# Mixture-of-experts hand-over of an adaptive-layernorm transformer block: routing of the first sixteen tiles placed inside the last batch's attention steps, the last eight tiles handled in pairs

## The reference, cut to what matters

```python
h = _layernorm(x) * (1 + ca) + sa
x = x + ga * _L0_attn_ref(h, ...)          # q, k, v; softmax; z @ W_o.T + b_o
h = _layernorm(x) * (1 + cb) + sb
x = x + gb * _L0_ffn_ref(h, ...)

# _L0_ffn_ref
score = softmax(xf @ Wg + bg); gate = max(score); idx = argmax(score)
pos = sum((cumsum(onehot(idx), axis=0) - 1) * onehot)   # rank within its expert, in token order
keep = pos < cap                                        # cap = 256
buf[idx, pos] = xf                                      # only where keep
h = relu(buf @ W1[e] + b1[e]);  y = h @ W2[e] + b2[e]
out = where(keep, y[idx, pos] * gate, 0)
```

## Time and profile before

| | us |
|---|---|
| time, median of 3 runs | 1383.31 (1381.31 to 1388.11) |
| the profiled execution | 1389.05 |
| its span | 1387.2 |
| PE busy | 1235.2 (89%) |
| DVE busy | 824.6 (59%) |
| ACT busy | 573.5 (41%) |
| POOL busy | 326.3 (24%) |
| chain that ended last | PE 67%, issue 11%, ACT 6%, DMA 5%, DVE 5%, POOL 3% |

### The profile page before, as it was taken

The page is one execution under the profiler, slowest core; times in us unless marked ns, Lnnn a source line. Parts: engine busy times, 40 slices in busy tenths (PEclk is TensorE's granted clock), DMA queues, the critical chain, the costliest instruction groups (busy, mean ns, idle before and its releaser), DMA issues.

```text
span 1387.2 us, 24033 instructions
## 1 busy us (share of the span) xinstructions
PE 1235.2 (89%) x7258; PEld 864.4 (62%) x7258; DVE 824.6 (59%) x2163; ACT 573.5 (41%) x1387; POOL 326.3 (24%) x488
## 2 busy tenths in 40 slices
PE   4588888888999999999999999999988529999995
PEld 1455555655666666666666666666656428888884
DVE  6356666666667766666667666666655623444443
ACT  2245555545555555555555555555540001111110
POOL 3111121111233332222333212222212520111111
PEclk7689999999999999999999999999999759999998
DMA  5311112111221222122122211212257852565630
GB/s 188 129 66 58 66 57 80 50 38 44 78 71 64 69 78 73 54 68 79 57 72 66 82 54 61 76 53 68 76 183 261 271 182 87 196 235 174 232 103 18
DMA packets 100150, 139.29 MB, mean 100 GB/s; under 512 B 9980, under 2 KB 71294, under 8 KB 99968
## 3 DMA queue, kind: packets, MB, share of 16 engines
q1 hardware_dynamic: 91536, 113.55, 24.9%
q10 hardware_dynamic: 4464, 16.25, 2.9%
q0 software_dynamic: 4096, 8.82, 1.6%
HBM read 94.50 MB, written 48.00 MB: 103 GB/s over the span
## 4 chain that ended last, share of the span: by engine, by line
PE 67%; issue 11%; ACT 6%; DMA 5%; DVE 5%; POOL 3%; SPq 2%; DVEq 0%; ACTq 0%; POOLq 0%
PE SC L676 16%; PE Z L694 14%; PE Z L841 8%; PE SC L815 8%; ACT E L876 5%; PE XA L648 5%; PE XA L726 4%; PE XA L658 3%; PE XB L658 3%; DMA xln<-in_x 3%; PE XB L648 2%; POOL Wvl L1371 1%; PE XB L713 1%; DMA out<-th 1%; POOL slots_s L1476 1%
## 5 line engine op out<-in xcount | busy, mean ns | idle before, releaser
L876 ACT ACTIVATE E<-SC,nm 128x512 f32<-128x512 f32 (+7 forms) x512 | 375.1, 739 | 426.3 <-DVE nm L1089 426.3
L1089 DVE CUSTOM_DVE_ANT_0 SC<-SC,mask 128x512 f32<-128x512 f32 (+7 forms) x512 | 375.9, 786 | 205.4 <-PE SC L676 204.2
L676 PE MATMUL SC<-XQ,XK 64*128 64x512 f32 (+3 forms) x2304 | 270.0, 366 | 55.7 <-ACT E L876 54.1
L676 PEld LDWEIGHTS SC<-XQ,XK 64*128 64x128 f32 x2304 | 187.7, 190 | 155.5 <-issue 138.6
L694 PE MATMUL Z<-E,vs 128*64 128x512 f32 (+3 forms) x1536 | 271.9, 496 | 3.0 <-DVE vs L1067 3.0
L694 PEld LDWEIGHTS Z<-E,vs 128*64 128x64 f32 x1536 | 100.3, 138 | 140.9 <-issue 128.1
L841 PE MATMUL Z<-W,hh 128*128 128x256 f32 x512 | 114.9, 383 | 2.2 <-DVE yb L1335 2.2
L815 PE MATMUL SC<-bT,W 128*128 128x256 f32 x512 | 114.7, 383 | 0.0
L815 PEld LDWEIGHTS SC<-bT,W 128*128 128x128 f32 x512 | 98.5, 193 | 13.7
L841 PEld LDWEIGHTS Z<-W,hh 128*128 128x128 f32 x512 | 97.3, 192 | 15.6 <-DVE yb L1335 2.6
L876 ACT ACTIVATION_READ_ACCUMULATOR E<-SC,nm 128x1 f32 x512 | 101.1, 197 | 0.0
(11 more groups left out here) (191 smaller groups left out, 1720.7 us busy)
## 6 DMA issues: line engine op xcount, KB each, us to landing
W<-in_w SPq DMA_DIRECT2D x32, 1024.0 KB, 8.4
z_s<-zs ACTq DMA_DIRECT2D x31, 512.0 KB, 2.6
zt<-z_s SPq DMA_DIRECT2D x24, 512.0 KB, 3.8
W<-in_wqk SPq DMA_DIRECT2D x33, 257.0 KB, 2.7
slots_s<-zt SPq DMA_DIRECT2D x16, 520.0 KB, 3.9
xb<-slots_s SPq DMA_DIRECT2D x16, 520.0 KB, 3.7
xb<-xh_s SPq DMA_DIRECT2D x24, 256.0 KB, 4.7
Wv<-in_wv SPq DMA_DIRECT2D x17, 256.0 KB, 2.7
```

What stands on the lines that cost most here:

```text
L676: last = pe.matmul(SC[h][:, at:at + z - a], XK[rows, ap, kp, lo:lo + P], XQ[rows, ap, qp, a:z], start=(t == 0), stop=(t == 2))
L876: act.activation(E[:, h, EOFF[kb]:EOFF[kb + 1]], SC[h][:, at:at + S - lo], ACT.Exp, bias=nm[:, h, kb:kb + 1], scale=-1.0, accum_out=rs[:, ...
L1089: dve.tensor_tensor_reduce(SC[h][:, at:at + S - lo], SC[h][:, at:at + S - lo], mask[:, 0:S - lo], 1.0, BIG, ALU.add, ALU.min, nm[:, h, kb: ...
```

## The change

1. `TAIL` is 8 and `T0` is 24: tile 23 is a normal `post` tile, in step 32. In that step `weigh(LATE)` comes after the tile's projection, and `project_out(0)` follows at once. ACT copies `Z` to `zs` in two halves; the first needs only key blocks 0 to 3.
2. Tiles 0 to 15 (lot 0) are routed inside steps 25 (`PICK`) and 26 (`RANK`) of batch 3: fifteen DVE instructions placed among the step's own, one exponential on ACT, sixteen running sums of `oh` on POOL (`sum_lot`, into `before`), and two matmuls into `Z` on PE (`lot_ranks`), one with `tri` and `oh`, one with `ones` and `before`, added up in PSUM. The DVE sums `base` are gone.
3. Their rows are loaded by SP and scattered by POOL in four rounds of four tiles: the loads at the end of steps 26 to 29, the scatters at the start of steps 27 to 30, through the two buffers `lead`.
4. Batch 3's steps are written out instead of looped.
5. The hand-over routes lot 1 (tiles 16 to 23) and then the last eight in four pairs (`route_tail`), each with its own two small matmuls and 16 DVE instructions. POOL's powers 0, 1 and 2 stand ahead of `lot_scatter`, and each pair is scattered when it is routed.
6. The product `boB * GA` is added to `x` by POOL (`gate_bias`) in step 31, so `norm_tail` has one DVE instruction fewer. The constants of routing are made ahead of the steps.

```diff
-TAIL = TPB + 1
+TAIL = TPB
-GROUPS = [(0, 1)] + [(1 + 2 * k, 2) for k in range(TPB // 2)]
-LOTS = [(0, 2 * TPB), (2 * TPB, 3 * TPB), (3 * TPB, NT)]
+GROUPS = [(2 * k, 2) for k in range(TPB // 2)]
+LOTS = [(0, 2 * TPB), (2 * TPB, 3 * TPB)]
+PICK, RANK = (B - 1) * PAIRS + 1, (B - 1) * PAIRS + 2
+ROUNDS, LEAD = 4, 4
...
-    (3, 0, 4, (0, 1), ("late", "att", "proj", "post")),
+    (3, 0, 1, (0, 1), ("late", "att", "proj", "post")),
+    (3, 1, 2, (0, 1), ("late", "att", "proj", "post")),
+    (3, 2, 3, (0, 1), ("late", "att", "proj", "post")),
+    (3, 3, 4, (0, 1), ("late", "att", "proj", "post")),
     (4, 0, 1, (0,), ("late", "att", "post")),
-    (4, 0, 1, (1,), ("late",)),
+    (4, 0, 1, (1,), ("late", "post")),
...
+                n = round_at(st, RANK)
+                if n is not None:
...
+                        sp.wait_ge(lead_sent, 16 * LEAD * n)
+                    for k in range(2):
+                        t = LEAD * n + LEAD // 2 * k
+                        sp.dma_start(lead[k][:, :, 0:2 * D], xh_s[t:t + LEAD // 2].rearrange("t p d -> p t d")).then_inc(lead_in, 16)
...
+                n = round_at(st, RANK + 1)
+                if n is not None:
...
+                    pool.wait_ge(lead_in, 32 * (n + 1))
...
+                            pool.indirect_dma_start(slots_s, bass.IndirectOffsetOnAxis(slot_u[:, t:t + 1], 0), lead[k][:, q, :], None,
+                                                    bounds_check=NE * CAP - 1, oob_is_err=False).then_inc(lead_sent, 16)
...
+                    if v == 1 and at_step(st, RANK):
+                        pe.wait_ge(s["zevac"], st.of("zevac", 1))
+                        lot_ranks(0, Z)
+                    if not st.has("att") and st.has("late") and v == 2:
+                        weigh(LATE)
+                        project_out(0)
...
+            tail_pow(0)
+            sum_lot(1)
             tail_pow(1)
-            scatter(1)
             tail_pow(2)
-            pool.wait_ge(routed, 2)
-            scatter(2, (0,))
+            lot_scatter()
             tail_pow(3)
-            scatter(2, (1,))
-            tail_pow(4)
...
+            for n in range(len(GROUPS)):
+                tail_scatter(n)
```

More of the change, by code:

```diff
@@ L313, in adaln_block @@
         b2B = sb("b2B", [P, NW, D])
[L314 to L318, removed]
         assert top[0] <= place["hTh"]
@@ L717, in step @@
                             project(*piece)
-                    if st.has("late") and v == 0:
+                    if st.has("late") and st.has("att") and v == 0:
                         weigh(LATE)
@@ L742, in _, with turn @@
             pe.wait_ge(s["zevac"], TOTAL["zevac"])
[L744 to L759, removed]
+            def turn(n):
                 u0, size = GROUPS[n]
                 pe.wait_ge(tail_h2, n + 1)
+                if n > 0:
+                    pe.wait_ge(tail_tT, n)
                 for q in range(size):
@@ L774, in gate_logits, with ranks @@
                 last.then_inc(tail_gates, 1)
[L776 to L785, removed]
-            ranks(0)
[L788 to L793, removed]
+            def ranks(n):
+                if n > 0:
+                    pe.wait_ge(routed, n)
+                pe.wait_ge(onehot, n + 1)
+                k0 = LOTS[1][1] - LOTS[1][0]
+                pe.matmul(XB[:, 0:2 * NE], tri[:, :], oh[:, 0:2, :].rearrange("p q e -> p (q e)"), start=True, stop=False)
+                pe.matmul(XB[:, 0:2 * NE], ones[:, :], before[:, k0:k0 + 2, :].rearrange("p q e -> p (q e)"),
+                          start=False, stop=True).then_inc(prefix_mm, 1)
+            project_out(1)
+            turn(0)
+            project_out(2)
+            gate(0)
+            lot_ranks(1, XA)
+            turn(1)
+            project_out(3)
+            gate(1)
+            turn(2)
+            ranks(0)
+            gate(2)
+            turn(3)
             ranks(1)
[L795 to L798, removed]
+            gate(3)
             ranks(2)
-            pe.wait_ge(routed, len(LOTS))
+            ranks(3)
+            pe.wait_ge(routed, len(GROUPS))
             xbT = [XA, XB]
@@ L1422, in step @@
                         split_values_weights(st.b * COUPLES + st.j + 2)
+                if at_step(st, PICK):
+                    sum_lot(0)
+                if st.has("att") and not st.has("proj"):
+                    gate_bias()
             minus_halves = mhalf[:, :].broadcast_to([P, TPB])
@@ new lines, in lot_scatter @@
+            def lot_scatter():
+                pool.wait_ge(lot_slotted, 2)
+                for half in range(2):
+                    ks = range(half * HS // 2, (half + 1) * HS // 2)
+                    t = LOTS[1][0] + ks[0]
+                    for k in ks:
+                        pool.wait_ge(hs_in[k], 16)
+                    pool.tensor_copy(hs[:, ks[0]:ks[0] + HS // 2, 2 * D:ROW], ext[:, t:t + HS // 2, :]).then_inc(ext_ok, 1)
+                    pool.wait_ge(ext_ok, half + 1)
+                    for k in ks:
+                        t = LOTS[1][0] + k
```

418 lines of the change are left out of this document (273 added, 145 removed).

## The result

| | before | after |
|---|---|---|
| time, median (from to), 11 runs each | 1384.68 (1379.92 to 1388.86) | 1379.29 (1375.24 to 1381.99) |
| the profiled execution | 1389.05 | 1377.41 |
| its span | 1387.2 | 1375.6 |

The ratio is 0.9956, with a 95% interval of 0.9939 to 0.9974, and the medians lie 5.4 us apart where 21.7 were forecast. Both kernels were timed again in a later session, and there the ratio was 0.9947 (0.9928 to 0.9967) and the medians 7.4 us apart (1384.82 and 1377.43).

What follows compares the result with a forecast made beforehand. PE was taken to bound batch 3's steps, and the hand-over alone the time from 1040 to 1139. Hand-over gain 23.5 us less 1.8 for the steps gave 21.7, from 1383.31 to 1361.6 us, range 1353 to 1372.

Steps and rivals of the forecast that it cites:

- The last weighted sum: End of attention on PE: 2.4 us instead of 3.96, with 4.0 as the other bound.
- PE's projection of tile 23: End of attention: 3.72 us at full clock, filling most of PE's 2.75 us gap, so tile 23 costs nothing there.
- the fourth power: Hand-over: it stands behind POOL's 12.2 us of `lot_scatter`, so DVE waits some 5 us for it.
- The three routings: Hand-over, pairs 1 to 3: 5.8, 4.7 and 4.0 us, together 14.5, bounds 12 and 19.
- From the last routing to the experts: End of the hand-over: two scatters remain instead of eight, 7.6 us less, so 8.7 instead of 16.33.
- rival 1: DVE slows POOL's scatters: mild 1370, strong about 1393; strong chance 0.05, mild within 0.18 shared with Rival 3.
- rival 2: Transfers of weights, reloads, scatters and output rows bind the hand-over: 1383 at half the rate; chance 0.05.
- Tile 23's turning and logits come between, 1.5 us ...; pair 1 ends at 1061.4.: PE's hand-over projections: after pair 0 ends at 1053.0, 1.5 us for tile 23, then pair 1 at 6.9 us.
- 5 x 0.2 = 1.0 us is paid almost in full: DVE, end of step 26: five `lot_slots` instructions delay step 27, costing 0.9 us, bounds 0 and 1.1.
- the base: Forecast time: median taken as 5.7 us below the profiled execution for outside reasons, so 1383.31 goes to 1361.6.
- Rival 3: Half the gain through a wait priced too low: gain 13, time 1370; chance 0.18 shared with rival 1's mild form.

Runs made afterwards that it cites:

- e4: Changed kernel with POOL's last eight scatters split into two halves and the fourth power between them; 1372.07 us, ratio 0.9915 to the kernel before.
- e1: Changed kernel with DVE's bias of tile 23's logits, which frees `XB`, moved ahead of `norm_tail(0)`; 1373.69 us, ratio 0.9908 to the kernel before.
- e5: Changed kernel with the edits of e1, e2 and e4 together; 1361.68 us, ratio 0.9836 to the kernel before.
- e2: Changed kernel with `lot_slots(0)` moved from step 26's end to the gap behind that step's logits; 1373.60 us, ratio 0.9916 to the kernel before.
- e3: Changed kernel with POOL's split of `Wv` in step 26 waiting for the slots, which stay in place; 1374.00 us, ratio 0.9923 to the kernel before.

## Why the prediction was wrong, step by step

**Held.** The last weighted sum took 2.38 us. PE's projection of tile 23 lay in the gap. `lot_scatter` took 12.2 us (1089.18 to 1101.38). DVE stood idle for the fourth power, 5.94 us for a forecast of some 5, and e4 got that back. The three routings took 14.5 us (1104.49 to 1119.0). From the last routing to the experts it was 8.7 us. The scatters in the steps took 0.97 to 1.24 us each, and `pt` did not wait for POOL, so rival 1 stayed away. The transfers did not bind (rival 2): SP issued the last weights at 1084, and 58 GB/s moved from 1100 to 1120.

**Failed: "Tile 23's turning and logits come between, 1.5 us ...; pair 1 ends at 1061.4."** The step priced PE's own instructions and not the wait behind them. PE may begin pair 1 only when `XB` is free, and DVE frees it behind `norm_tail(0)`. All the parts were at hand: pair 0 ends at 1053.0, `norm_tail` is 3.0 + 0.84 + most of 2.3 us, so `XB` comes free about 1059, and pair 1 could not begin at 1054.5. The time between the last logits of step 31 and the first expert was forecast at 76 us and is 83.1 (1044.59 to 1127.66); e1 took 7.0 off. (The prediction calls these logits, at 1040.0, PE's last matmul of attention; the weighted sum behind them ends at 1046.7. The 99 and the 76 us count from the same mark, so the sum is not touched.)

**Mis-sized: "5 x 0.2 = 1.0 us is paid almost in full".** The steps were to pay 1.8 and paid 5.2. The five instructions did lie on the path, but took 2.26 us, because POOL's split of `Wv` ran beside them, and the idle time that followed cost PE its clock. The profile of before has POOL's copy right beside DVE's start at 893.98, and at the start of the kernel it even has the price. On POOL, then the summary of line `L1026` on DVE (minimum, median and maximum in ns):

```profile
27.15 1.26 POOL L1371 TENSOR_TENSOR Wvl<-Wv,Wvh 128x512 fp32r<-128x512 f32 x1
894.20 0.61 POOL L1369 CAST Wvh<-Wv 128x512 fp32r<-128x512 f32 x1 [11.87 <-DVE vs L1067]
...
L1026 DVE TENSOR_SCALAR V<-V,E x8: 340/346/1422, 25.5 to 28.7; 128x256 f32<-128x256 f32 x8
```

The instruction of 1422 ns is the one that starts at 27.14, beside POOL's subtraction. I looked at the pair DVE and POOL only for what DVE would do to the scatters. 0.4 us more lies in step 30 (30.47 us), where PE stands idle for 0.35 us waiting for ACT; no experiment touched it.

**Failed: the base.** "The median of the runs is 5.7 us below it, for reasons outside the steps and the hand-over as far as the rows tell." Some 2.0 of that (330.17 against the mean of four, 328.2) was inside the hand-over. A forecast made in one execution's rows carried that execution's late reload over as a gain.

**The sum, again.** 21.7 forecast, less 7.0 for `XB`, 3.4 for the steps, 2.0 for the base, leaves 9.3; the profiled executions from the store on show 328.2 - 319.5 = 8.7. The medians show 5.4 and 7.4. Of the rest, some 2.0 lie ahead of step 24: its store comes at 808.1 to 811.2 in the four executions of before (mean 809.2), and at 808.2 to 813.1 in the eight of kernels with the change (mean 811.3). The differences arise in the first 350 us, where the granted clock is still under 1.00 (0.78 to 0.83 in the first 100); from there to step 24 all keep the same pace at 1.00. Whether the change has a part in it, by the constants made there, or whether it is chance, stays open.

Rival 3 (half the gain, 1370) was the nearest, for one of its three reasons, the steps (6 us, measured 5.2); the range, down to half the gain, ended at 1372. That e5 measured 1361.68, next to the forecast of 1361.6, is chance: the forecast had DVE's wait for the fourth power in it, and e4 took that away. The change with the first two places alone mended would by the same rows be at some 1366 (1377.4 - 7.0 - 4.0), which was not run.

## What to carry to other kernels

When work is pulled forward on one engine, list for its next instruction every semaphore that it waits for and look up **where in the giver's stream** the release stands; a small read-out of a shared bank goes ahead of long work that nobody waits for. Where small VectorE instructions are put in series with the path, look at what GpSimd does in that very microsecond, as well as at what they do to GpSimd. And take a stretch from several executions before its length goes into a sum: here one stretch varied by 3.5 us, two thirds of the gain that was measured.

## What the runs showed of the hardware

A GpSimd instruction can hold up a VectorE instruction for its whole rest. The conversion `L1181`, 128x16, took 1.13 us beside POOL's subtraction of 128x512 and ended with it; in e2, away from it, the same row is 0.18 and in e3 0.17. `L1179` took 0.56 beside POOL's copy and 0.17 without. The Trainium skill ("SBUF — State Buffer", Who interferes with whom) says that the two share one pair of ports as an exclusive lock, and that of whoever comes second "the other **fully blocks** (not throttle)"; it counts `tensor_scalar` among those that can take that pair. The trace agrees in the row of `L1181`, which ends 0.02 us after POOL's subtraction; `L1179` is not a `tensor_scalar`, and it ends 0.03 us after POOL's copy all the same. The profile of before shows the same at 27.14 us: a `tensor_scalar` of 128x256, 0.35 us in the median, takes 1.42 beside POOL's subtraction. The large reductions right behind (`L1235`) took 1.22 us beside POOL at 896.19, and 1.23 at 927.88, where POOL did nothing.

The idle time that brings PE's clock down was 2.36 us at the turn of a step, behind steps in which PE was full (0.50 in the window 902 to 904, and 1.6 us more for step 28); 1.11 us at the same place left it at full clock. What an idle time costs is not fixed: behind the same 3.29 us in step 31, the scores took 2.29 us in both executions of after and 1.31 in that of e4.

The sixteen scatters of POOL in steps with a busy DVE took 0.97 to 1.24 us: the strong factor that rival 1 feared is in none of them.
